# Mixture-of-experts stage: outputs scattered to a row per token and choice, second half routed behind the first half's blocks

## The reference, cut to what matters

```
xn    = layernorm(x)                         # per token, 256 features
prob  = softmax(xn @ Wr)                     # 8 experts
top 2 of prob, renormalised to sum 1 -> w1, w2
y(e)  = (silu(xn @ Wg[e]) * (xn @ Wu[e])) @ Wd[e]
out   = x + w1 * y(e1) + w2 * y(e2)
```

## Time and profile before

| | us |
|---|---|
| median of 3 runs | 3052.18 (3052.17 to 3054.16) |
| the profiled execution's own time | 3063.06 |
| its span, from first to last instruction | 3060.9 |
| expert stage, by its first normalise to the end | 2552.5 to 3060.9 |
| clearing: POOL's memset to DVE's first instruction after the barrier | 40.4 to 53.5 |

### The profile page before, as it was taken

The page is one execution under the profiler, slowest core; times in us unless marked ns, Lnnn a source line. Parts: engine busy times, 40 slices in busy tenths (PEclk is TensorE's granted clock), DMA queues, the critical chain, the costliest instruction groups (busy, mean ns, idle before and its releaser), DMA issues. The chain is left out here.

```text
span 3060.9 us, 69490 instructions
## 1 busy us (share of the span) xinstructions
PE 2449.2 (80%) x22172; PEld 1532.3 (50%) x22172; DVE 2149.1 (70%) x6125; ACT 1103.0 (36%) x2488; POOL 1045.4 (34%) x1535
## 2 busy tenths in 40 slices
PE   2555447999999974999888887599999997568882
PEld 1333324555555534999766665244444445434441
DVE  4999986787777866666589997577788874223343
ACT  1222213555555542222233332355566652012220
POOL 3444442222222214666544443222222220440124
PEclk8676768999999986999999998699999996579996
DMA  6000014443444410000000000533333330122333
GB/s 229 1 0 0 0 43 89 91 90 84 86 83 88 90 26 1 0 0 0 1 1 0 0 0 0 163 94 97 94 91 90 95 85 2 62 90 69 100 111 114
DMA packets 260951, 180.24 MB, mean 59 GB/s; under 512 B 36032, under 2 KB 255072, under 8 KB 259840
## 3 DMA queue, kind: packets, MB, share of 16 engines
q1 hardware_dynamic: 249920, 157.93, 20.3%
q0 software_dynamic: 6784, 17.02, 1.8%
q10 hardware_dynamic: 4160, 4.19, 0.5%
HBM read 94.10 MB, written 83.36 MB: 58 GB/s over the span
## 5 line engine op out<-in xcount | busy, mean ns | idle before, releaser
L736 ACT ACTIVATE xattn_pr<-ps 128x384 f32<-128x384 f32 (+1 forms) x1024 | 537.0, 544 | 489.1 <-PE ps L506 232.8
L610 DVE TENSOR_REDUCE xattn_mx<-ps 128x2 f32<-128x512 f32 x512 | 342.2, 679 | 127.8 <-PE ps L472 120.9
L485 PE MATMUL ps<-xattn_qp,xattn_kp 128*128 128x192 bf16 (+1 forms) x2048 | 416.0, 264 | 2.1 <-DMA xattn_qp<-xattn_mrow 1.8
L472 PE MATMUL ps<-xattn_kp,xattn_qp 96*128 96x192 bf16 (+1 forms) x2048 | 372.6, 264 | 34.4 <-DMA xattn_kp<-xattn_rows 29.2
L606 DVE CUSTOM_DVE_ANT_0 xattn_masked<-ps,xattn_band 128x192 bf16<-128x192 f32 x1024 | 323.7, 353 | 100.4 <-issue 45.1
L485 PEld LDWEIGHTS ps<-xattn_qp,xattn_kp 128*128 128x128 bf16 x2048 | 164.0, 98 | 282.3 <-ACT xattn_pr L736 152.5
L506 PE MATMUL ps<-xattn_pr,xattn_vs 128*32 128x256 f32 (+1 forms) x4096 | 303.4, 368 | 0.0
L506 PE MATMUL ps<-xattn_pr,xattn_ones 128*32 128x256 f32 (+1 forms) x4096 | 303.2, 368 | 0.0
L472 PEld LDWEIGHTS ps<-xattn_kp,xattn_qp 96*128 96x128 bf16 x2048 | 189.0, 99 | 68.7 <-issue 22.1
L2415 POOL TENSOR_TENSOR attn_kmask<-attn_k,const_sb 128x1024 f32<-128x1024 f32 x64 | 154.0, 2425 | 189.9 <-ACT attn_k L2292 189.9
L488 PE MATMUL ps<-xattn_band,xattn_ident 128*128 128x192 bf16 x1024 | 211.7, 247 | 0.0
(11 more groups left out here) (306 smaller groups left out, 4797.2 us busy)
## 6 DMA issues: line engine op xcount, KB each, us to landing
xattn_rows<-xattn_parts SPq DMA_DIRECT2D x128, 192.0 KB, 2.0
xattn_qp<-xattn_rows SPq DMA_DIRECT2D x256, 96.0 KB, 2.8
xattn_kp<-xattn_rows SPq DMA_DIRECT2D x256, 96.0 KB, 3.2
xattn_rows<-xattn_parts SPq DMA_DIRECT2D x128, 128.0 KB, 1.9
moe_xb<-moe_rows_in SPq DMA_DIRECT2D x78, 128.0 KB
moe_rows_out<-moe_yb SPq DMA_DIRECT2D x78, 128.0 KB
moe_rows_in<-region_zero SPq DMA_DIRECT2D x8, 1024.0 KB, 10.6
xattn_rows<-xattn_parts SPq DMA_DIRECT2D x128, 64.0 KB, 1.7
```

The source lines that it names most:

```text
L472: mm = nc.tensor.matmul(ps[:, BANK_S + j % RING, mt * D:mt * D + width], qp[u][s][0:R_MAX, h, mt * P:(mt + 1) * P], kp[u][s][0:R_MAX, h, l ...
L485: mm = nc.tensor.matmul(out, kp[u][s][:, h, nt * P:(nt + 1) * P], qp[u][s][:, h, lo:lo + width], start=True, stop=not banded)
L610: ins = nc.vector.tensor_reduce(mx[s][:, h * NT:(h + 1) * NT], ps[:, BANK_S + j % RING, :].rearrange("p (m n) -> p m n", m=NT), AX.X, ALU.max)
L736: nc.scalar.activation(out, src, ACT.Exp, scale=HD ** -0.5).then_inc(exped, 1)
```

## The change

1. A row of `moe_rows_in` grows from 256 to 258 floats (1,032 bytes): the features, then the row number to which the expert's output is to go, then the choice's weight. So each pair has two rows in SBUF, `row[0]` and `row[1]`; DVE normalises into `row[0]`, and ACT copies it to `row[1]` (`copy_row`, 32 new ACT instructions). DVE writes token numbers once (4 small copies).
2. `clear_regions` writes zeros with a spare row number in each row, so that unused rows send their output to a spare place. POOL writes the numbers into the zero tile; this is done in 3 rounds, and before rounds 2 and 3 POOL waits until the DMAs of the rounds before have landed. SP issues 2 DMAs of 1.72 MB a round.
3. After a block, DVE makes an int32 row number (`to`), multiplies the result by the weight in `keep_y`, and POOL scatters the 128 rows with one indirect DMA (`send`, 78 in all) straight to the row of its token and choice. SP's 78 stores and POOL's 64 gathers go.
4. The ring is RB = 5. `load_block(n)` now waits until the output of block n-5 has been sent and has landed (`sent`), where it waited for PE's turn of the buffer's previous block.
5. PE's order in iteration n: turn hidden n, turn block n+3, gate and up of n+2, down of n. DVE's `keep_y(n)` comes in iteration n+1, behind `make_hidden(n+2)`.
6. Part 1 is routed beside part 0's blocks, two pairs an iteration from n = 0 to 9, its groups' DVE and PE work at n = 5 to 13, `count` at 14, `block_table` at 15, and its 32 scatters two to an iteration at n = 16 to 31.
7. When a part is done, SP loads its outputs in token order (`load_outputs`: 8 DMAs of 512 KB) over the rows of `row`, DVE adds them to x in place (2 `tensor_tensor` a pair), and SP stores four pairs at a time (`store_out`). For part 0 the loads stand at n = 44 in SP's order, the sums at n = 53 to 68, and the four stores behind the loads of n = 62, 66, 70 and 74.

```
 def clear_regions(core, ctx):
+            for q in range(parts):                       # parts = 3
+                wait(g, cleared, 16 * PARTS_R * q)
+                spare = core.c[:, C_SPARE + q * CLEAR:C_SPARE + (q + 1) * CLEAR]
+                nc.gpsimd.tensor_copy(zero[:, :, D:D + 1], ...).then_inc(made, 1)
...
+            for q in range(parts):
+                sp.wait_ge(made, q + 2)
+                for h in range(PARTS_R):
+                    sp.dma_start(to, zero[:]).then_inc(cleared, 16)
...
 # SP
-                    wait(sp, xb_turned, n - RB + 1)
+                    wait(sp, sent[n % RB], 16 * (n // RB))
                     sp.dma_start(xb[n % RB][:], x_in[part][b * P:(b + 1) * P, :]).then_inc(xb_in[n % RB], 16)
-                def store_block(part, b):
...
+                def load_outputs(part):
+                    for r in range(RB):
+                        sp.wait_ge(sent[r], 16 * uses((part + 1) * BLOCKS, r))
+                    for q in range(QUARTERS):
+                        for k in range(2):
+                            sp.dma_start(row[k][:, part * PP + q * EACH:..., 0:D], of_plane[:, q * EACH:..., :]).then_inc(y_in[part][q], 16)
+                for n in range(N):
+                    load_block(n)
+                    if n == BLOCKS + 5:
+                        load_outputs(0)
+                    if n - 6 in SUMMED and SUMMED[n - 6] % EACH == EACH - 1:
+                        store_out(0, SUMMED[n - 6] // EACH)
+                load_outputs(1)
...
 # PE
+                for n in range(N):
+                    turn_hidden(n)
+                    if n + 3 < N:
+                        turn_block(n + 3)
+                    if n + 2 < N:
+                        e[n + 2] = gate_up(n + 2)
+                    down_product(n, e.pop(n))
+                    for p in LOGITS.get(n, []):
+                        logit_product(p)
+                    for p in TURNED.get(n, []):
+                        turn_x(p)
+                    if n in PLACES:
+                        places(PLACES[n])
+                    if n == COUNT:
+                        count(1)
...
 # DVE
-                    nc.vector.tensor_copy(yb[n % RB][:], ps[:, BANK_D, 0:D]).then_inc(y_kept, 1)
+                    nc.vector.tensor_copy(to[n % RB][:], xb[n % RB][:, D:D + 1]).then_inc(to_made, 1)
+                    nc.vector.tensor_scalar(yb[n % RB][:], ps[:, BANK_D, 0:D], xb[n % RB][:, D + 1:D + 2], None, ALU.mult).then_inc(y_kept, 1)
...
 # POOL
+                for n in range(N):
+                    send(n)
+                    if n == MOVED:
+                        g.wait_ge(tabled, 2 * TABLE)
+                    if MOVED <= n < MOVED + PP:
+                        scatter(PP + n - MOVED)
```

More of the change, by code:

```diff
@@ L1335 @@
 ROWS = BLOCKS * P
+ROW = D + 2
+CLEAR = 13
 def clear_regions(core, ctx):
     nc = core.nc
[L1341 to L1344, removed]
+    x_in = [nc.dram_tensor(f"moe_rows_in{h}", (ROWS, ROW), F32).ap() for h in range(PARTS_R)]
+    y_out = [nc.dram_tensor(f"moe_rows_out{h}", (2 * REGION + ROWS, D), F32).ap() for h in range(PARTS_R)]
+    zero = core.sb("region_zero", [P, CLEAR, ROW], ctx=ctx)
     made, cleared = nc.alloc_semaphore(name="region_zero_made"), nc.alloc_semaphore(name="region_cleared")
-    starts = range(0, ROWS, P * each)
+    parts = ROWS // (P * CLEAR)
     with nc.Block() as block:
@@ L1384, in sem @@
             return core.sem(f"{name}_{n}")
-        xn = sb("xn", [P, PAIRS, D])
+        row = [sb(f"row{k}", [P, PAIRS, ROW]) for k in range(2)]
         xt = [sb(f"xt{u}", [P, NT, P]) for u in range(2)]
@@ L1458, in store_out @@
[L1458 to L1469, removed]
@@ L1475, in _ @@
+                load_outputs(1)
+                for q in range(QUARTERS):
+                    store_out(1, q)
+                sp.wait_ge(left, 16 * QUARTERS * PARTS_R)
             @block.tensor
@@ L1555, in expert_of @@
                 def expert_of(n):
-                    part, b = divmod(n, BLOCKS)
+                    part, b = of(n)
                     if b == 0:
@@ L1562, in _ @@
                 pe.wait_ge(*landed)
-                for p in range(PAIRS):
-                    if p + 1 < PAIRS:
+                for p in range(PP):
+                    if p + 1 < PP:
                         turn_x(p + 1)
@@ L1782, in _ @@
-                make_hidden(0, 0)
-                for n, (part, b) in enumerate(blocks()):
-                    if n + 1 < N:
-                        make_hidden(*divmod(n + 1, BLOCKS))
-                    keep_y(part, b)
-                    for p in sums_after(part, b):
-                        add_up(p)
-                for p in range(PAIRS - PP, PAIRS):
+                block_table(0)
+                make_hidden(0)
+                for n in range(N):
+                    if n + 1 < N:
+                        make_hidden(n + 1)
+                    if n > 0:
+                        keep_y(n - 1)
+                    for p in NORMED.get(n, []):
+                        normalise_x(p)
+                    if n in EXPS:
+                        less_maximum(EXPS[n])
+                    if n in RANKS:
+                        ranks(RANKS[n])
+                    if n in CHOICES:
+                        choices(CHOICES[n])
+                    if n == COUNT + 1:
+                        block_table(1)
+                    if n in SUMMED:
+                        add_up(SUMMED[n])
@@ L1790, in _ @@
+                keep_y(N - 1)
+                for p in range(PP, PAIRS):
                     add_up(p)
```

285 lines of the change are left out of this document (150 added, 135 removed).

## The result

The changed kernel takes 3175.07 us (median of 4, 3168.04 to 3180.47), the kernel before 3052.18 (4 runs of each, 3045.99 to 3054.16): ratio 1.0405, 95% interval 1.038 to 1.043, slower. Forecast were 3088 and, with the rivals, a range of 3046 to 3128. The side was right, the size not: +123 us instead of +36. The profiled span is 3173.9 us for 3060.9, 113 more.

A forecast was written before the change was run, and what follows sets the result against it. PE was busy 80% of the span, an average over stages with different limits. Terms 16 - 21 + (14 + 13 + 16 + 11 + 7) - 20 = +36 took the median from 3052.2 to 3088 us; own range 3064 to 3112, with rivals 3046 to 3128.

The forecast's parts named there:

- a: Clearing at the start: rounds wait for earlier transfers to land, delaying every engine's time mixing; +16 us, +12 to +20.
- b: Start of the expert blocks: without part 1's routing on PE the first block waits for its load alone; -21 us.
- c: Block period: loop from output's send to load five blocks later sets 4.4 us instead of 3.82; +14, bounds 4.1 to 4.8.
- d: Part 1's routing between part 0's blocks adds work on PE and DVE; +13 us, range 6 to 20.
- e: Part 1's scatters beside the blocks disturb them by 1 us a block; +16 us, least 0, most 48.
- rival 2: Part 1's scatters, one pair at a time beside blocks, disturb nothing; 3072 us, chance 0.20.
- f: Part 0's outputs: loads at n = 44 delay load 45, +11 us; the four stores delay later loads, +7.
- g: End after the last down: 31 us where 50.8 were, without POOL's gathers; -20 us, bounds 27 and 40.
- Rival 1: In the blocks PE, not the send-to-load loop, sets the period, 3.35 us a block; 3016 us, chance 0.12.
- rival 3: Part 1's scatters disturb the blocks beside them as before, 48 us in all; 3120 us, chance 0.20.
- Rival 4: The 1,032-byte rows make each indirect DMA slower, say by half of 0.96 us; 3133 us, chance 0.08.

The follow-up runs named there:

- e11: Changed kernel with three zero tiles instead of one for the clearing, so no copy of row numbers waits for a transfer: 3171.00 us, ratio 1.0377.
- e18: Changed kernel with eight aligned slots, three zero tiles, part 0's outputs loaded in quarters, 56 unused columns, but part 1 routed ahead of the blocks: 2926.01 us, ratio 0.9751.
- e1: Changed kernel with eight slots instead of five, outputs written in place over their rows: 3011.15 us, ratio 1.0028 to the kernel before.
- e2: Changed kernel, five slots, but a block's load waits for the multiplication that reads the slot, not for the output's send: 3020.17 us, ratio 1.0061.
- e4: Changed kernel with two extra unused products ahead of the waiting turn, once per two blocks from block 22, keeping PE busy: 3141.70 us, ratio 1.0455.
- e16: Changed kernel with extra products keeping PE busy, the expert's number read early and plain stores for indirect sends: 3081.20 us, ratio 1.0082.
- e15: Changed kernel with eight aligned slots, early expert number, three zero tiles, part 0's outputs loaded in quarters, 56 unused columns: 2968.75 us, ratio 0.9708.
- e5: The changed kernel again, unaltered, traced on one chip with the kernel before: 3167.23 us, ratio 1.0376.
- e6: The kernel before again, unaltered, traced on the same chip as the changed kernel's repeat: 3051.03 us.

## Why the prediction was wrong

- **a, +16: measured +9.6.** Right in kind: the waits of 9.6 us by their rows. A round takes 9.8 us and not 10.7, and SP is done with the third round (62.60) 0.8 us behind POOL's copy and not 3.6. The stated least of +12 was a slip: two transfers of 8.2 us with the rest of the working give +10.7. e11 confirms the cause.
- **b, -21: measured -20.5** (132.8 to 112.3 us from cross attention to first down). Right in size; e18 shows that the reason (PE has no part 1 work) holds only where ACT is late beside the scatters.
- **c, 4.4 us a block, the step that failed: measured 5.92.** The loop was named rightly and is the bound (e1, e2). The term that was mis-sized is PE's part, from turn to down: forecast 3.2 us, measured 5.77, which is 2.6 of the 3.0 us by which a pair is longer. I took it at full speed, though by my own sum PE would idle some 2 us of a pair ahead of it (8.8 less twice 3.35), and rows of the kernel before show both levels (3.77 us for gate and up, which b used). With the clock kept up it is 3.97 (e4) and 3.02 (e16). POOL's wake is the second, 0.76 us for 0.3; the send's landing, 2.45 for 2.4, and the load were right. My upper bound of 4.8 moved only the links, not what a wait does to the engine behind it. 77 x 1.52 = 117 us too little. That e16 comes out at the forecast's 4.4 is in part luck: its sends are plain stores, 0.4 us quicker than what the forecast took, and that makes up for POOL's and DVE's longer links.
- **d, +13 and e, +16: measured nothing on top of c** (blocks 0 to 16 take 5.8 us each, 16 to 32 6.0, 44 to 74 5.92). The longer wait hides them. With the loop gone they are there: in e1 blocks 0 to 16 take 5.3 us where later ones take 3.0, 37 us; e, from 3.0 us a block, 4 us in e1 and 24 in e15, the chip with the late ACT. So that rival 2 (e is 0) fits the changed kernel is the loop's doing and not for the reason it gave.
- **f, +11 and +7: measured +12 and 0.** Blocks 40 to 44 take 35.8 us where four steady ones take 23.7; the stores cost nothing that shows. Load 45 is issued at 2936.81 and its rows are turned at 2944.93, 8.1 us for 2.1. By the Trainium skill (*DMA: Bandwidth & Descriptors*, "Queues, rings and completion order") descriptors are consumed in ring order on each DMA engine. The trace agrees: the load takes 6 us more with the outputs' loads ahead of it.
- **g, -20: measured -24.9**, 26.0 us from the last down's end, under the forecast's bound of 27.
- **Not in the sum: +16.2** in the cross attentions and what lies between (28 in e5 and e6), from 71 columns in a table. The prediction gave the tiles' own addresses no term. The Trainium skill (*DMA: Bandwidth & Descriptors*, "How a descriptor splits into AXI transactions") says that a transaction must start at a multiple of 256 bytes, and that bytes fetched ahead of an unaligned start still cost. The traces agree in that 512-byte packets are quickest at such a multiple, 32 ns; that they take 38 ns at 64 mod 256 and 42 at 32 mod 64 the section doesn't tell apart.
- By the measured terms: 9.6 + 16.2 - 20.5 + 132.6 - 24.9 = 113.0 us, the spans' difference. **Rival 1** is refuted (PE sets the pace only where the loop is gone), **rival 3** (e is 48) too: blocks 16 to 32 take 96.2 us, 1.5 more than sixteen later ones. **Rival 4** is refuted for the scatters: with 1,032-byte rows POOL still takes 0.96 us each.

## What to carry to other kernels

When a buffer's release moves from the reader to the end of a write, work out the whole loop through DMA, queue and engine, and charge the engine's part at the clock that its rows show behind a wait of that length; then ask whether one more slot or an earlier release takes the loop away, as one changed wait did here (e2, 3.48 us a block for 5.92). A tile or table made longer moves every tile behind it: look at the packet times of stages that the change doesn't touch. Ask of moved work what covers it where it stands now; here, on the quicker chips, it was free, and was moved to where it costs 30 us; on the slower ones the two orders are equal.

## What the runs showed of the hardware

- After a wait of 3.42 us on PE the granted clock was 0.50, and gate and up took 3.78 us for 1.88; keeping PE busy in that wait with unused products held it at 0.98 and made the kernel faster, work added.
- A tile's address sets the time of its DMA packets: 512 bytes take 32 ns at a multiple of 256, 38 at 64 mod 256, 42 at 32 mod 64.
- SP issued the load that waits for an indirect write of 128 rows 2.42 us after POOL's start (median), and 2.00 us after it for a plain store.
- Chips differ by 50 us for the kernel before (3051 to 3059 us, and 3001 to 3003). On the slower ones ACT was up to 15.8 us late beside POOL's scatters; in the blocks and the routing of six kernels on the two quicker ones it never was by over 2.5 us, and two orders of the same work that are equal on a slower chip differ by 36 us there.
